# A gated linear-attention head loop: three projections moved between the halves of a blocked inverse, and two engines' loops written out

## The reference

```python
mixed = silu(conv4(x @ w_qkv))          # a causal convolution over 4 tokens, per channel
q, k, v = split(mixed); z = x @ w_z; beta = sigmoid(x @ w_b); g = ...
def step(Sm, inp):                      # over the tokens
    Sm = Sm * exp(g)
    delta = (v - k @ Sm) * beta
    Sm = Sm + outer(k, delta)
    return Sm, q @ Sm                   # q and k are l2-normalized
on = rmsnorm(o * silu(z)) * norm_w
out = on @ w_out
```

## Time and profile before

| | |
|---|---|
| median of 3 runs | 3094.16 us (3086.99 to 3102.05) |
| the profiled execution's own time | 3097.86 us |
| its span | 3096.1 us |
| the 64 steps, from the first joining level to the last | 122.27 to 2690.13 us |
| PE busy | 2761.4 us, 89% |
| DVE busy | 2385.2 us, 77% |
| ACT busy | 1765.9 us, 57% |
| POOL busy | 1236.7 us, 40% |
| TensorE's granted clock, mean | 0.963 |
| the same from 776 to 2690 us | 0.99 |

### The profile page before, as it was taken

How to read it: one execution, slowest core, us unless ns; L and a number is a source line. 1 busy time by engine, 2 the same in 40 slices (tenths; PEclk the granted TensorE clock), 3 DMA queues, 4 the chain that set the end, 5 groups by cost and what they waited for, 6 DMA issues and landing times. The chain is left out here.

```text
span 3096.1 us, 129193 instructions
## 1 busy us (share of the span) xinstructions
PE 2761.4 (89%) x52495; PEld 2287.1 (74%) x52496; DVE 2385.2 (77%) x5142; ACT 1765.9 (57%) x5625; POOL 1236.7 (40%) x1120
## 2 busy tenths in 40 slices
PE   2599989898999999999999999999999999967888
PEld 1477777777787878787878787878788888744555
DVE  7577787777877777777887878777778787638996
ACT  1366666666666666666666666666666666521111
POOL 4555555655333333333333333333333333335620
PEclk8799999999999999999999999999999999988999
DMA  4211111101111111111110111111111111163311
GB/s 170 73 52 55 42 41 31 31 27 29 44 30 42 30 44 30 44 30 44 30 44 30 44 30 37 29 37 34 39 34 41 34 41 34 34 228 98 115 63 41
DMA packets 94202, 155.58 MB, mean 50 GB/s; under 512 B 17238, under 2 KB 61829, under 8 KB 92403
## 3 DMA queue, kind: packets, MB, share of 16 engines
q1 hardware_dynamic: 69779, 112.45, 12.2%
q0 software_dynamic: 12288, 24.19, 2.5%
q10 hardware_dynamic: 11520, 10.49, 1.0%
HBM read 115.18 MB, written 41.29 MB: 51 GB/s over the span
## 5 line engine op out<-in xcount | busy, mean ns | idle before, releaser
L1278 DVE SCALAR_TENSOR_TENSOR p_y<-p_xr,p_cw,p_y 128x512 f32<-128x512 f32 x768 | 673.4, 885 | 44.3 <-ACT p_y L1027 23.8
L1085 ACT ACTIVATE p_Xs<-p_psI 128x256 f32<-128x256 f32 (+1 forms) x386 | 160.3, 415 | 523.0 <-PE p_psI L762 451.0
L714 PE MATMUL p_psF<-xnS,p_w_hl 128*128 128x512 f32 x1536 | 433.4, 419 | 21.1 <-PEq L586 21.1
L1504 POOL TENSOR_TENSOR p_E<-p_E,p_sj 128x512 f32<-128x512 f32 x128 | 131.8, 1050 | 744.2 <-DVE p_sj L1305 744.2
L714 PEld LDWEIGHTS p_psF<-xnS,p_w_hl 128*128 128x128 f32 x1536 | 278.0, 195 | 74.6 <-issue 21.7
L1323 DVE TENSOR_TENSOR p_ATP<-p_psF,p_E 128x512 f32<-128x512 f32 x256 | 166.5, 687 | 180.6 <-PE p_psF L749 171.6
L1512 POOL TENSOR_TENSOR p_M<-p_ATc,p_masks 128x512 f32<-128x512 f32 x128 | 170.4, 1336 | 308.4 <-ACT p_ATc L1065 308.4
L771 PE MATMUL p_psI<-p_Xs,p_DTc 32*32 32x32 f32 x16384 | 213.6, 196 | 66.6 <-issue 64.6
L762 PEld LDWEIGHTS p_psI<-p_Dc,p_M 32*32 32x32 f32 x16384 | 174.4, 107 | 130.9 <-issue 122.8
L771 PEld LDWEIGHTS p_psI<-p_Xs,p_DTc 32*32 32x32 f32 x16384 | 177.0, 107 | 121.0 <-issue 106.1
L762 PE MATMUL p_psI<-p_Dc,p_M 32*32 32x32 f32 x16384 | 205.5, 195 | 60.0 <-DVE p_DTc L1341 35.2
(11 more groups left out here) (328 smaller groups left out, 6541.1 us busy)
## 6 DMA issues: line engine op xcount, KB each, us to landing
p_ab<-decays SPq DMA_DIRECT2D x64, 512.0 KB, 5.3
p_w_raw<-in_w_in SPq DMA_DIRECT2D x17, 768.0 KB
expert_out<-p_ye ACTq DMA_DIRECT2D x80, 128.0 KB, 2.2
p_wgu<-in_w_gu SPq DMA_DIRECT2D x56, 176.0 KB
expert_in<-p_zero SPq DMA_DIRECT2D x16, 512.0 KB, 9.7
p_xe<-expert_in SPq DMA_DIRECT2D x56, 128.0 KB
p_wd<-in_w_down SPq DMA_DIRECT2D x56, 88.0 KB
p_wout<-in_w_out SPq DMA_DIRECT2D x16, 256.0 KB
```

Source lines behind the costliest of these rows:

```text
L714: m = pe.matmul(b4(psF[f % 2][:, :]), w_hl[:, wp, kt, ty * P:(ty + 1) * P], xnS[:, xp, kt, :].rearrange("p (b t) -> p b t", b=B)[:, :, c * ...
L1085: act.activation(dst, src, ACT.Copy).then_inc(s["xs" if l < 5 else "join_xs"], 1)
L1278: m = dve.scalar_tensor_tensor(y[:, ty, :, :], xr[:, ty, :, tap:tap + P], cw[:, ty, tap:tap + 1], y[:, ty, :, :], ALU.mult, ALU.add)
```

## The change

Four things are done together.

- PE: `project` 0 (keys) no longer opens a step. It stands in the step before, between `turn_out` and `level_y` 4. `project` 3 moves from before `level_x` 1 to behind `level_y` 1. `project` 2, which was split in two around `level_x` 2, stands whole behind it. The gate's second sequence moves from before `solve` to behind it. Both `within` now stand between the halves of level 1.
- ACT: `out_squares` 0 moves from before `inverse_copy` 2 to behind the copy of the expert's up product, directly ahead of `out_squares` 1. The copy of the expert's down product moves ahead of `inverse_copy` 4.
- DVE: `outputs` 1 moves ahead of `level` 1.
- The loops over `kh` of ACT and DVE are written out, with constants in place of registers.

```diff
             def step(kh, c):
-                project(kh, c, 0)
                 project(kh, c, 1)
                 expert(kh, c, EX_IN)
...
                 turn(kh, c, QUERIES_T, lambda b: kq[c % 2][:, b, Q_, :], "silu", 2)
-                project_z(kh, c, (0, 1))
+                project_z(kh, c, (0,))
                 solve(kh, c - 1)
-                project(kh, c, 3)
+                project_z(kh, c, (1,))
                 level_x(kh, c, 1)
                 within(kh, c - 1, 0)
+                within(kh, c - 1, 1)
                 level_y(kh, c, 1)
-                within(kh, c - 1, 1)
-                project(kh, c, 2, (0, 3))
+                project(kh, c, 3)
                 level_x(kh, c, 2)
-                project(kh, c, 2, (3, 6))
+                project(kh, c, 2)
                 expert(kh, c, EX_UP)
...
                 level_x(kh, c, 4)
                 turn_out(kh, c - 1)
+                if c < NC - 1:
+                    project(kh, c + 1, 0)
+                elif kh < HK - 1:
+                    project(kh + 1, 0, 0)
                 level_y(kh, c, 4)
 
+            project(0, 0, 0)
             for kh in range(HK):
...
                 evacuate(kh, c, 3)
-                out_squares(kh, c - 1, 0)
                 inverse_copy(kh, c, 2)
                 evacuate(kh, c, 2)
                 expert(kh, c, EX_UP)
+                out_squares(kh, c - 1, 0)
                 out_squares(kh, c - 1, 1)
                 inverse_copy(kh, c, 3)
+                expert(kh, c, EX_DOWN)
                 inverse_copy(kh, c, 4)
-                expert(kh, c, EX_DOWN)
...
-            with heads_loop(nc, "heads_act", mybir.EngineType.Activation, HK) as (kh, announce):
+            for kh in range(HK):
                 for c in range(NC):
-                    if c == NC - 1:
-                        announce()
                     step(kh, c)
...
                 outputs(kh, c - 1, 0)
+                outputs(kh, c - 1, 1)
                 level(kh, c, 1)
-                outputs(kh, c - 1, 1)
                 conv(kh, c, 3, (0, 1))
...
-            with heads_loop(nc, "heads_dve", mybir.EngineType.DVE, HK) as (kh, announce):
+            for kh in range(HK):
+                count[0] = 0
                 for c in range(NC):
-                    if c == NC - 1:
-                        announce()
                     step(kh, c)
```

## The result

The kernel after takes 3153.4 us (median of 4 runs, 3147.3 to 3155.8), the kernel before beside it 3096.5: ratio 1.0193, interval 1.0173 to 1.0213. It is 57 us slower where 25 were forecast. The profiled execution took 3147.3 us (span 3145.5), 49.4 more than the one of before.

What follows compares the result with a forecast made beforehand. PE, busy 89% of the span, was taken as the bound, its waits ended by ACT's and DVE's chains. Late heads +29 us and early heads -4 made +25: 3119 us predicted, forecast's own range 3105 to 3140, overall 3072 to 3155.

Steps and rivals of the forecast that it cites:

- stretch A: Step from turn of the keys to turn of the queries: nothing moved, unchanged at 39.7 us a head.
- early heads: First four heads, where POOL scatters tokens: -1 us a head (-3 to +2) from 163.6, -4 us in all.
- load of the activation table: ACT's 1.28 us load, 16 times, goes; costed at nothing because the keys wait for DVE's convolution; 20 us if on the path.
- Stretch B: Turn of the queries to level 1: DVE's transposes limit the gain from the removed projection; 19.55 us a head.
- Stretch C: Level 1 to end of level 4: later squares and row scales set level 4; 19.05 us a step, 76.2 a head.
- The stops: PE's instruction stream running dry inside L771, in second halves of levels: fall from 64.6 us to under 15.
- Stretch D: End of level 4 to turn of the keys: the keys' projection leaves, the 6.2 us chain remains; 26.0 us a head.
- POOL holds DVE: Rival, chance 0.08: POOL's state decay slows DVE's taps, row scales start at 12.1 in chunks 2 and 3; +51 us, 3170.
- Written out: ACT's and DVE's loops replaced by constants: only the loop's edge, 0.41 us of idle DVE a head, goes.
- shorter links: Rival, chance 0.17: without register instructions ACT and DVE answer 0.03 to 0.1 us earlier, 0.9 us a step, -58 us: 3061.
- the stops stayed: Rival, chance 0.09: stops of about 1 us a step remain in level 1 to level 4; +0.5 x 64, 3151 us.
- an even trade: Rival, chance 0.24: half the shorter-links gain, or level 1 to 4 a half microsecond shorter; 3090 us, no difference.

Runs made afterwards that it cites:

- e11: Kernel after, with the queries' projection computed twice in chunk 1 to fill PE's wait: 3215.7 us against 3227.5 for the kernel after beside it, 1.0107 to before.
- e1: Kernel before, with only ACT's and DVE's steps written out for all 16 heads in place of loops: 3078.9 us, ratio 0.9930 to before.
- e9: Kernel after, with both the first copied value's projection (project 3) and the first set of output squares back in their old places: ratio 1.0036 to before.
- e12: Kernel before, ACT and DVE written out, with four of six products of the next keys' projection between the halves of level 4: ratio 0.9900 to before.
- e13: Kernel before, ACT and DVE written out, with three of six products of the next keys' projection between level 4's halves, second timing: ratio 0.9894 to before.

## Why the prediction was right or wrong

Right in direction and in most of the steps of a late head, too small by 32 us of 57. What failed are three terms: stretch A taken as unchanged, the early heads taken as 1 us shorter each, and the load of the activation table costed at nothing.

- **Stretch B**: 19.55 predicted, 19.73 measured. Level 1 starts 0.14 us behind DVE's transposes.
- **Stretch C**: 76.2 and 0.4 for the stops predicted, 76.9 measured by the prediction's own mark. On its way, counted from the end of level 1's first half, the squares start at 7.86 (7.85 predicted), the row scales at 10.33 (10.45), level 4 at 14.2 (14.4), and from there to its end it is 4.1 in most steps (3.95). The stops, predicted under 15 us in all, are 25.9. In the second halves of level 4 they are gone (21.6 us in the late heads before, 0.5 after); 12.3 us stay in level 3's. Where one falls there, PE comes later and a wait of about 0.2 us is left ahead of level 4; elsewhere it is mostly 0.8, and 1.8 in chunk 0, where 1 and 2 to 3 were predicted. The mean is 0.7.
- **Stretch D**: 26.0 predicted, 25.5 measured.
- **Stretch A failed.** "Nothing in it is moved", 39.7: measured 40.51, as the clock falls after the keys' wait of chunk 1. The prediction named that wait, 2 us, as a sign that it was right, and gave it no price beyond itself. +0.8 in 12 heads, +1.0 in four: 14 us. By e11 it goes when that wait is filled.
- **The early heads failed.** -1 us a head predicted, +4.1 measured, 20 us off in four heads. 4 us of it are in the 14 above. The rest is in stretch C. Before the change an early head's C was 4.2 us longer than a late one's. The sum let that shrink to "some waits", 0.75 us; it grew to 5.6. Two thirds of it stand in chunks 2 and 3, where POOL's work falls on DVE's taps. A step of chunk 2:

```profile
556.71 2.52 POOL L1541 TENSOR_TENSOR p_OG<-p_O,p_zs 128x512 f32<-128x512 f32 x2
...
558.45 4.13 DVE L1280 SCALAR_TENSOR_TENSOR p_y<-p_xr,p_cw,p_y 128x512 f32<-128x512 f32 x2 [1.65 <-ACT p_y L1031]
559.19 2.05 POOL L1534 TENSOR_TENSOR p_St<-p_St,p_gk 128x512 f32<-128x512 f32 x2
...
563.36 0.16 DVE L1405 TENSOR_TENSOR p_sm<-p_so,p_xq 128x8 f32<-128x8 f32 x1
...
563.54 1.02 PE L762 MATMUL p_psI<-p_Dc,p_M 32*32 32x32 f32 x64 [1.39 <-DVE p_DTc L1343]
```

  The two taps overlap POOL's back-to-back products (L1541, L1534) and last 4.13 us (1.54 in chunks 0 and 1). The subtraction of level 2 stands behind them in DVE's list, so PE waits 1.39 us for it ahead of level 3. The row scales start 11.2 us behind level 1, hardly later than in a late step (11.0): the hold reaches level 4 by way of level 3, which ends later and with more stops (9 us in the 16 early steps). In chunk 3 the row scales are late too, at 12.2; that is 11.5 by the count of the prediction, whose rival *POOL holds DVE* had 12.1 in both chunks. But the hold is not new: before the change the taps of chunk 2 took 5.6 us, more than now. They ran from 4.3 to 9.9 us behind level 1, and now from 6.3 to 10.4. That POOL holds DVE is read from the overlap; no kernel took POOL's work away, so it was not tried. In the late heads the rival decided nothing (1.5 to 2.5 us for the taps, and the squares end later).
- **Written out failed too**, to the other side: costed at 0.41 us a head, measured by e1 at 20 us in all. The load of the activation table was costed at nothing, as the keys wait for DVE's convolution; the rows show PE waiting behind that load for the copy of the queries' projection, 1.12 us in the one shown. It is luck that this term and the two above have opposite signs: without it the forecast would have missed by more. The Trainium skill, Runtime: NRT & Kernel Launch, "Instruction fetch mechanics", says that a taken branch breaks the prefetch. The 0.41 us of idle DVE at the edge, gone in e1, agree with it in kind; how much of stretch D's 0.7 to 1.3 us an edge is the branch and how much the load, no run shows.
- **The sum.** In the profiled pair: late heads 12 x 2.84 = 34 (29 predicted), early heads 4 x 4.1 = 16 (-4 predicted), 50 in all against 25, and 49.4 measured. The medians differ by 57 and not by 49, since the profiled execution of after was the shortest of its runs. Set against e1 instead of before, the moves alone cost 74 us by medians of two sets, and 81 by the ratios. What the small swaps (both `within` together, the gate's second sequence behind `solve`, `outputs` 1 and the expert's copy earlier) do was not tried one by one.

Of the rivals, shorter links is refuted by e1 and the stops stayed in part; an even trade holds for the keys' projection by itself.

## What to carry to other kernels

A filler moved between two halves is worth what it covers at the new place less what it uncovers at the old one. Put no more there than the other engine's chain leaves room for: half of the projection won 1.1%, with writing out (0.7% of it by itself), and the whole, in e9, lost that again. Where a stream that runs dry and a chain of another engine end at nearly the same place, count in how many steps each ends last before pricing either: 0.46 us of the chain came back whole, and of 0.76 only 0.32. Price a new wait of TensorE of 2 us not only by its length but by the clock behind it.

## What was unexpected of the hardware

After waits of 1.8 to 1.9 us ahead of stretch A, the late heads lost some 1.4 us (in single cases 3.0) to the lower clock in 5 to 10 cases of 12, by the kernel; after waits of up to 1.2 us (before, e11, e12, e13) in none. Adding 24 us of products to the kernel after did not make it slower (1.0107 against 1.0134). The same kernel's four heads with scattering took 167.7 us each on one chip and 180.4 on another, where the late heads differed by 0.6.
